# Attention sums one step behind the scores, two activation places, half-step waits, on one Trainium2 core

## The chip, the core and the metric

The kernel runs on one core of a Trainium2 chip. Its engines run side by side and meet at semaphores: TensorE (PE) multiplies matrices into PSUM, ScalarE (ACT) computes activations, VectorE (DVE) does element-wise work and reductions, GpSimd (POOL) does small work and issues some DMAs, and SyncE (SP) issues the others. The metric is the device time of one execution in microseconds (us), and less is better.

## The reference, cut to what matters

One sequence of 2048 rows of 128 features passes an attention layer and a feed-forward layer, each with a residual sum and a layer norm.

```python
x_proj = silu(x @ W1 + b1); u, v, q, k = split(x_proj, 4)      # 16 heads of 8
scores = einsum('bqhd,bkhd->bhqk', qh, kh)
attn = silu(scores) / S                                        # no softmax: S = 2048
av = einsum('bhqk,bkhd->bqhd', attn, vh)
y = layernorm(av * u, gamma, beta) @ W2 + b2                   # x = layernorm(x + y)
h = silu(fp4_linear(x, w_gate)) * fp4_linear(x, w_up)          # 352 features
x = layernorm(x + fp4_linear(h, w_down))                       # fp4: blocks of 16, quantised
```

So 16 x 2048 x 2048 scores have to pass through a SiLU, which only ACT computes, and every one of them is then multiplied with V.

## The kernel before

**Steps.** The queries are cut into ten chunks (`WIDTHS`): six of 256 columns, then four of 128. A step is one block of 128 keys against 1024 columns of scores for each of two halves: for a wide chunk that is two of the four head groups `m`, for a narrow chunk all four. There are 256 steps (`STEPS`), numbered from 0; steps 0 to 191 are wide and 192 to 255 narrow. A wide chunk has 32 steps, a narrow one 16 (`BEGIN` holds their first steps).

**A step on each engine.** PE computes the scores of the step in two half steps (`scores`), each 128x1024 values into a pair of PSUM banks. There are three pairs (`SB`), so half step n waits until ACT has finished half step n-3. ACT turns each pair by one ACTIVATE (line 656) into a place of the tile `attn`, which has `RING` = 3 places of one whole step. PE then multiplies `attn` with a padded V (`times_v`) and adds into one accumulator bank per chunk (`AV`). A step's sum (its "sums" below) is 16 recorded matmuls in a wide chunk and 32 in a narrow one.

**Order on PE.** It is written out (lines 562 to 569): the scores of step `at`, the sums of step `at - LAG` with `LAG` = 2, then at most one job. `times_v` waits once, for both activations of its step (line 464), which two steps behind have long been done.

**Jobs.** The projections of later K, Q, V and u columns and the transposes of the weights are put at fixed steps (`PREP_AT`). Behind the attention of a chunk the other layers of its 128-row tiles are six jobs per tile: `y`, `xqT`, `gate`, `up`, `hqT`, `down` (`TILE_AT`, `EVEN`, `ODD`). Between them DVE normalises and quantises, POOL computes the square root, and ACT runs one SiLU per tile. In a wide chunk tile jobs `down` of an even tile and `y` of an odd one stand one step after the other, as do `hqT` and `down` of an odd tile. The four narrow chunks hold the jobs of tiles 10 to 14, at bases that contain `LAG`. The last tile is computed after the last sums, in the tail, where PE multiplies zeros between its pieces (`keep_warm`). Jobs use the accumulator bank that is not in use (`spare_bank`, which also contains `LAG`), and the sums of a chunk's first step wait for the last job in their bank (`wait_spare`).

Of the kernel before, what the change touches and what calls it, by code (L numbers as in the profile page):

```python
# [12 lines left out]
P = 128  # L13
# [26 lines left out]
def build(nc, x, W1, b1, W2, b2, gamma, beta, w_gate, w_up, w_down, out):  # L40
# [8 lines left out]
    M = 4  # L49
    FEAT = 3  # L50
    PARTS = 5
    TERMS = len(Q_TERMS)
    RING = 3
    SB = 3
    LAG = 2
    WARM_UP = 6
    KEEP_WARM = {"y": 5, "xqT": 27, "gate": 2, "hqT": 22, "down": 2}
    FT = [(0, P), (P, P), (2 * P, FF - 2 * P)]
# [8 lines left out]
    Q0 = [sum(WIDTHS[:c]) for c in range(len(WIDTHS))]  # L67
# [5 lines left out]
    def ms(c, g):  # L73

        per = CH // WIDTHS[c]
        return M_ORDER[g * per:(g + 1) * per]

    AV = [6 + c % 2 for c in range(len(WIDTHS))]

    def spare_bank(at):  # L80

        return 13 - AV[STEPS[at - LAG][0]] if at >= LAG else 7


    PREP_AT = {1: ("v", 1), 3: ("k", 1280), 6: ("v", 2), 8: ("k", 1792), 10: ("v", 3), 12: ("u", 0),
               14: ("q", 256), 16: ("u", 1), 18: ("q", 512), 20: ("u", 2), 22: ("q", 1024), 24: ("u", 3),
               26: ("q", 1536), 28: ("w2", 0), 30: ("gate", 0), 32: ("up", 0), 33: ("down", 0)}

    TAIL = KT - 1
    WIDE, DENSE = KT - 6, KT - 2  # L90
# [3 lines left out]
    for t in range(WIDE, DENSE):  # L94
        TILE_AT[t] = (BEGIN[WIDE // 2 + 1] + LAG + 12 * (t - WIDE),
                      {"y": 0, "xqT": 4, "gate": 5, "up": 7, "hqT": 10, "down": 11})
    TILE_AT[DENSE] = (BEGIN[-2] + LAG, {"y": 0, "xqT": 4, "gate": 6, "up": 8, "hqT": 12, "down": 13})
    JOB_AT = {at: (kind, i, None) for at, (kind, i) in PREP_AT.items()}
# [17 lines left out]
    with ExitStack() as ctx:  # L116
        def sb(name, shape, dt=F32):
            return ctx.enter_context(nc.sbuf_tensor(name, shape, dt))

        def sem(name):  # L120
            return ctx.enter_context(nc.semaphore(name))
# [43 lines left out]
        k_stack = sb("k_stack", [P, SLOTS, S], BF16)  # L165
        q_stack = sb("q_stack", [P, SLOTS, S], BF16)
        attn = sb("attn", [P, RING, 2, 2, CH])
        zu = sb("zu", [P, CH])
# [31 lines left out]
        scores_ready, attn_ready = sem("scores_ready"), sem("attn_ready")  # L200
# [168 lines left out]
        def _(pe):  # L369
            def mm(to, lhsT, rhs, start=True, stop=True):  # L370
                return pe.matmul(to, lhsT, rhs, start=start, stop=stop, skip_group_check=True)  # L371
# [63 lines left out]
            def wait_stacked(c, g, i):  # L435

                if c == g == 0 and ("k", i * P) in unit_no:
                    wait_stack(pe, unit_no[("k", i * P)])
                if g == i == 0 and ("q", Q0[c]) in unit_no:
                    wait_stack(pe, unit_no[("q", Q0[c])])  # L440

            def scores(at):
                c, g, i = STEPS[at]
                w = WIDTHS[c]
                wait_stacked(c, g, i)
                for a in range(2):
                    n = 2 * at + a
                    bank = 2 * (n % SB)
                    if n >= SB:
                        pe.wait_ge(attn_ready, n - SB + 1)  # L450
                    else:
                        pe.wait_ge(head_act, max(head_last[bank], head_last[bank + 1]) + 1)
                    for k, m in enumerate(ms(c, g)):
                        for half in range(2):
                            rows = slice(64 * half, 64 * half + 64)
                            last = mm(ps[:, bank + half, k * w:(k + 1) * w],
                                      k_stack[rows, M * a + m, i * P:(i + 1) * P],
                                      q_stack[rows, M * a + m, Q0[c]:Q0[c] + w])
                    last.then_inc(scores_ready, 1)

            def times_v(at):
                c, g, i = STEPS[at]
                w = WIDTHS[c]
                pe.wait_ge(attn_ready, 2 * (at + 1))
                if c == g == 0 and i % TPC == 0:
                    pe.wait_ge(v_padded, i // TPC + 1)
                if g == i == 0:
                    wait_spare(AV[c], at + LAG)
                for k, m in enumerate(ms(c, g)):
                    for a in range(2):  # L470
                        for half in range(2):
                            cols = slice(32 * (2 * half + a), 32 * (2 * half + a) + 32)
                            last = mm(ps[cols, AV[c], 0:w], v_pad[:, i, m, cols],
                                      attn[:, at % RING, a, half, k * w:(k + 1) * w],
                                      start=(m == M_ORDER[0] and i == 0), stop=(m == M_ORDER[-1] and i == KT - 1))
                last.then_inc(av_done, 1)
# [8 lines left out]
            def wait_spare(bank, at):  # L485

                ks = [k for k, (a, b) in enumerate(zip(sorted(JOB_AT), JOB_BANK)) if b == bank and a < at]
                if ks:
                    wait_job(ks[-1])
                else:  # L490
                    pe.wait_ge(head_act, head_last[bank] + 1)

            def job(at):
# [5 lines left out]
                else:  # L499
                    pe.wait_ge(head_act, head_last[bank] + 1)  # L500
                if at >= BEGIN[1] + LAG:

                    pe.wait_ge(av_taken, STEPS[at - LAG][0])
                if tile is not None:
# [57 lines left out]
            for at in range(len(STEPS)):  # L562
                scores(at)
                if at >= LAG:
                    times_v(at - LAG)
                if at in JOB_AT:
                    job(at)
            for at in range(len(STEPS) - LAG, len(STEPS)):
                times_v(at)
# [29 lines left out]
        def _(act):  # L599
            def silu(to, frm, **kw):  # L600
                return act.activation(to, frm, ACT.Silu, **kw)  # L601
# [47 lines left out]
            for at in range(len(STEPS)):  # L649
                for a in range(2):  # L650
                    n = 2 * at + a
                    act.wait_ge(scores_ready, n + 1)
                    if a == 0 and at >= RING:
                        act.wait_ge(av_done, at - RING + 1)
                    b = 2 * (n % SB)
                    silu(attn[:, at % RING, a, :, :], ps[:, b:b + 2, :]).then_inc(attn_ready, 1)
                    if a == 0 and at - 1 in JOB_AT:
# [16 lines left out]
        def _(dve):  # L674
# [78 lines left out]
            def take_av(c):  # L753
# [3 lines left out]
                for tile in range(TAIL):  # L757
                    if chunk_of(tile) == c - 1:
                        dve.wait_ge(job_made, job_no[("y", 0, tile)] + 1)
                dve.scalar_tensor_tensor(out=zu[:, 0:w], in0=ps[:, AV[c], 0:w], scalar=1.0 / S,  # L760
                                         in1=uT[:, Q0[c]:Q0[c] + w], op0=ALU.mult, op1=ALU.mult).then_inc(av_taken, 1)
# [198 lines left out]
```

## Time and profile before

| | |
|---|---|
| median of 3 runs | 524.06 us (523.19 to 524.69) |
| the profiled execution | 523.96 us |
| its span (first to last instruction) | 522.2 us |
| busy: ACT | 490.9 us, 94% |
| busy: PE | 502.7 us, 96% |
| busy: weight loads (PEld) | 265.5 us, 51% |
| busy: DVE | 212.3 us, 41% |
| busy: POOL | 56.6 us, 11% |
| granted PE clock, mean | 0.996 |

The span leaves 1.8 us of the execution outside. Busy time on PE is modelled at the end of each matmul, so starts of instructions are the safer numbers there. A timeline view merges a run of equal instructions into one row and gives the idle time before it in brackets. Its ACT rows contain activations that overlap at their edges. Of the page's chain of waits, ACT has 50% and PE 32%, and its issue share is 13%.

### The profile page before, as it was taken

Reading aid. Unit: us, or ns where it says so; the run is one execution under the profiler, and the core shown is the slowest. Engines: PE = TensorE matmul, PEld = TensorE weight load, DVE = VectorE, ACT = ScalarE, POOL = GpSimd, SP = SyncE. Lnnn points to the kernel's source line nnn. Section 1 sums busy time; section 2 is a strip of 40 time slices with the busy share of each in tenths; the row PEclk is TensorE's granted clock in tenths of the full one; section 3 lists DMA queues with packets and bytes.
Section 4 is the critical chain, followed back from the end, with each engine's and each line's share of the span. In section 5 each row is a group of like instructions: output and inputs, shape, how many; then the busy total and the mean of one; then the engine's idle time right before and its main releaser. Section 6 shows DMA issues by size and latency. Waiting matters only on the chain.

```text
span 522.2 us, 20050 instructions
## 1 busy us (share of the span) xinstructions
PE 502.7 (96%) x9054; PEld 265.5 (51%) x9056; DVE 212.3 (41%) x624; ACT 490.9 (94%) x557; POOL 56.6 (11%) x148
## 2 busy tenths in 40 slices
PE   8899999999999999999999999999999999999996
PEld 5454334444444434444443444444477777777753
DVE  5447742332433432243433432243434354544344
ACT  5899999999999999999999999999999999999920
POOL 7700001010010101001010100001010110101010
PEclk9899999999999999999999999999999999999999
DMA  7831450000000000000000000000000000000000
GB/s 186 203 94 48 107 141 4 1 8 3 6 3 1 8 2 8 3 1 8 2 8 1 8 1 8 3 3 8 1 9 4 9 9 5 9 3 9 4 8 6
DMA packets 15155, 12.38 MB, mean 24 GB/s; under 512 B 1783, under 2 KB 14718, under 8 KB 15070
## 3 DMA queue, kind: packets, MB, share of 16 engines
q1 hardware_dynamic: 14088, 9.44, 6.9%
q0 software_dynamic: 688, 1.40, 1.1%
q8 instruction: 71, 1.16, 0.9%
q10 hardware_dynamic: 294, 0.26, 0.2%
q14 instruction: 14, 0.11, 0.1%
HBM read 1.92 MB, written 1.05 MB: 6 GB/s over the span
## 4 chain that ended last, share of the span: by engine, by line
ACT 50%; PE 32%; issue 13%; DVE 2%; POOL 1%; DMA 1%; POOLq 0%; DVEq 0%; ACTq 0%
ACT attn L601 50%; PE ps L371 30%; PE ps L385 2%; DMA q_stack<-parts 1%; POOL rstd_b L359 1%; PE ps L414 0%; DVE stats_b L764 0%; ACT feat L601 0%; POOL ve_b L358 0%; DVE mv_b L766 0%; ACT v_sb L601 0%; DVE x_b L769 0%; DVE x1p_b L774 0%; DVE xn_b L742 0%; DVE xn_b L743 0%
## 5 line engine op out<-in xcount | busy, mean ns | idle before, releaser
L601 ACT ACTIVATE attn<-ps 128x1024 f32<-128x1024 f32 x512 | 478.8, 1191 | 3.4 <-PE ps L371 3.1
L371 PE MATMUL ps<-attn,v_pad 128*32 128x256 f32 (+1 forms) x5120 | 274.5, 341 | 0.4 <-ACT attn L601 0.3
L371 PE MATMUL ps<-q_stack,k_stack 64*128 64x256 bf16 (+1 forms) x2560 | 174.1, 251 | 10.9 <-ACT attn L601 1.4
L371 PEld LDWEIGHTS ps<-attn,v_pad 128*32 128x32 f32 x5120 | 132.4, 109 | 80.4 <-issue 38.9
L371 PEld LDWEIGHTS ps<-q_stack,k_stack 64*128 64x128 bf16 x2560 | 78.5, 94 | 135.1 <-ACT attn L601 90.6
L358 POOL TENSOR_TENSOR ve_a<-mv_a,eps_col 128x1 f32<-128x1 f32 x24 | 4.6, 191 | 264.2 <-DVE mv_a L766 264.2
L814 DVE TENSOR_TENSOR gate_a<-gate_a,ps 128x352 f32<-128x352 f32 x8 | 4.2, 522 | 55.4 <-PE ps L371 55.4
L358 POOL TENSOR_TENSOR ve_b<-mv_b,eps_col 128x1 f32<-128x1 f32 x24 | 4.6, 192 | 175.6 <-DVE mv_b L766 175.6
L814 DVE TENSOR_TENSOR gate_b<-gate_b,ps 128x352 f32<-128x352 f32 x7 | 3.7, 522 | 47.0 <-PE ps L371 47.0
L371 PE MATMUL ps<-zeros 128*128 128x512 bf16 (+1 forms) x63 | 16.1, 403 | 1.3 <-DVE zeros L835 1.2
L701 DVE CAST parts<-feat 128x512 bf16<-128x512 f32 (+1 forms) x10 | 3.7, 373 | 26.8 <-ACT feat L601 26.8
L359 POOL TENSOR_TENSOR rstd_a<-ve_a,minus_half 128x1 f32<-128x1 f32 x24 | 13.2, 552 | 1.9
L359 POOL TENSOR_TENSOR rstd_b<-ve_b,minus_half 128x1 f32<-128x1 f32 x24 | 13.2, 551 | 1.9
L371 PE MATMUL ps<-wgate_t,xqT 128*32 128x352 f32 (+1 forms) x122 | 12.5, 460 | 0.2 <-ACT xqT L662 0.2
L371 PE MATMUL ps<-wup_t,xqT 128*32 128x352 f32 (+1 forms) x122 | 12.4, 459 | 0.0
L769 DVE TENSOR_SCALAR x_a<-x1p_a,mv_a,rstd_a 128x128 f32<-128x128 f32 x16 | 5.5, 347 | 15.0 <-POOL rstd_a L359 15.0
L769 DVE TENSOR_SCALAR x_b<-x1p_b,mv_b,rstd_b 128x128 f32<-128x128 f32 x16 | 5.5, 346 | 15.0 <-POOL rstd_b L359 15.0
L822 DVE COPY hqT_a<-ps 128x256 f32<-128x256 f32 x8 | 3.4, 425 | 19.2 <-PE ps L385 19.2
L828 DVE TENSOR_TENSOR x1p_a<-ps,x_a 128x128 f32<-128x128 f32 x8 | 2.3, 292 | 21.2 <-PE ps L371 21.2
L371 PEld LDWEIGHTS ps<-zeros 128*128 128x128 bf16 x65 | 6.4, 102 | 8.7 <-issue 1.7
L764 DVE BATCH_NORM_STATS2 stats_a<-ps 128x6 f32<-128x128 f32 x8 | 2.4, 298 | 19.1 <-PE ps L371 19.1
L601 ACT ACTIVATE feat<-ps,b_col 128x512 f32<-128x512 f32 (+1 forms) x10 | 7.5, 746 | 2.5 <-PE ps L371 2.5
(152 smaller groups left out, 346.9 us busy)
## 6 DMA issues: line engine op xcount, KB each, us to landing
q_stack<-parts SPq DMA_DIRECT2D x18, 128.0 KB, 2.4
k_stack<-parts SPq DMA_DIRECT2D x15, 128.0 KB, 3.5
x_sb<-in_L_attn_x SPq DMA_DIRECT2D x3, 256.0 KB, 4.6
k_stack<-zeros SPq DMA_DIRECT2D x6, 128.0 KB, 4.8
q_stack<-zeros SPq DMA_DIRECT2D x6, 128.0 KB, 2.9
k_stack<-parts SPq DMA_DIRECT2D x9, 64.0 KB, 2.1
q_stack<-parts SPq DMA_DIRECT2D x9, 64.0 KB, 2.9
out<-x_a SPq DMA_DIRECT2D x8, 64.0 KB, 1.6
```

Source lines behind the costliest of these rows:

```text
L358: link(pool.tensor_tensor(r.ve[:, :], r.mv[:, which, 1:2], eps_col[:, :], ALU.add))
L359: pool.tensor_tensor(r.rstd[:, which:which + 1], r.ve[:, :], minus_half[:, :], ALU.pow).then_inc(rstd_ready, 1)
L371: return pe.matmul(to, lhsT, rhs, start=start, stop=stop, skip_group_check=True)
L385: return pe.transpose(ps[0:m, bank, a:a + n], src[:, 0:m], ident[0:n, 0:n])
L601: return act.activation(to, frm, ACT.Silu, **kw)
L701: dve.tensor_copy(p[:, 0, :], f).then_inc(split_done, 1)
L764: dve.bn_stats(r.stats[:, :], src)
L769: return dve.tensor_scalar(to, src, r.mv[:, which, 0:1], r.rstd[:, which:which + 1], ALU.subtract, ALU.mult)
L814: dve.tensor_tensor(r.gate[:, :], r.gate[:, :], ps[:, bank, 0:FF], ALU.mult).then_inc(job_by_vec, 1)
L822: dve.tensor_copy(r.hqT[:, 0:2, :].rearrange("p t n -> p (t n)"), ps[:, bank, 0:2 * P])
L828: dve.tensor_tensor(r.x1p[:, :], ps[:, bank, 0:D], r.x1[:, :], ALU.add).then_inc(job_by_vec, 1)
```

## The change

`LAG` goes from 2 to 1 and `RING` from 3 to 2. The new function `group` lets a half step hold half of the `m` with both halves `b` of the stacks, where before it held all `m` with one. With that a half step of `attn` feeds a complete half of the step's sums, and `times_v` waits for each half of the activations by itself. Three weight transposes now stand at steps 30, 31 and 32 in place of 30, 32 and 33. Through `LAG` the jobs of tiles 10 to 14 stand one step earlier, and the bank of a job is chosen for the step before it.

```diff
-    RING = 3
+    RING = 2
     SB = 3
-    LAG = 2
+    LAG = 1
...
+    def group(c, g, a):
+
+        some = ms(c, g)
+        return [(m, b) for m in some[a * len(some) // 2:(a + 1) * len(some) // 2] for b in range(2)]
+
...
-               26: ("q", 1536), 28: ("w2", 0), 30: ("gate", 0), 32: ("up", 0), 33: ("down", 0)}
+               26: ("q", 1536), 28: ("w2", 0), 30: ("gate", 0), 31: ("up", 0), 32: ("down", 0)}
...
-                    for k, m in enumerate(ms(c, g)):
+                    for k, (m, b) in enumerate(group(c, g, a)):
                         for half in range(2):
                             rows = slice(64 * half, 64 * half + 64)
                             last = mm(ps[:, bank + half, k * w:(k + 1) * w],
-                                      k_stack[rows, M * a + m, i * P:(i + 1) * P],
-                                      q_stack[rows, M * a + m, Q0[c]:Q0[c] + w])
+                                      k_stack[rows, M * b + m, i * P:(i + 1) * P],
+                                      q_stack[rows, M * b + m, Q0[c]:Q0[c] + w])
...
-                pe.wait_ge(attn_ready, 2 * (at + 1))
...
-                for k, m in enumerate(ms(c, g)):
-                    for a in range(2):
+                for a in range(2):
+                    pe.wait_ge(attn_ready, 2 * at + a + 1)
+                    for k, (m, b) in enumerate(group(c, g, a)):
                         for half in range(2):
-                            cols = slice(32 * (2 * half + a), 32 * (2 * half + a) + 32)
+                            cols = slice(32 * (2 * half + b), 32 * (2 * half + b) + 32)
```

The order of instructions on PE shows it in three places. In these rows `q_stack,k_stack` are scores, `attn,v_pad` are sums, and `attn_ready` is ACT's count of finished half steps. The first place is step 1 and the start of step 2, before; `w1_sb,xT` and `b1v_parts,ones_bf16` are the projection of V for keys 512 to 1023:

```order
29 L371 MATMUL ps<-q_stack,k_stack 128x256 [waits attn_ready]
30 L371 MATMUL ps<-q_stack,k_stack 128x256 x3
31 L371 MATMUL ps<-w1_sb,xT 32x128 [waits head_act]
32 L371 MATMUL ps<-w1_sb,xT 32x128 x15
33 L371 MATMUL ps<-b1v_parts,ones_bf16 32x512 x4
34 L371 MATMUL ps<-q_stack,k_stack 128x256 [waits attn_ready,stacked_by_pool2,stacked2]
```

The same place on PE in the changed kernel:

```order
30 L376 MATMUL ps<-q_stack,k_stack 128x256 x3
31 L376 MATMUL ps<-attn,v_pad 32x256 [waits attn_ready,head_act,v_padded]
32 L376 MATMUL ps<-attn,v_pad 32x256 x3
33 L376 MATMUL ps<-attn,v_pad 32x256 [waits attn_ready]
34 L376 MATMUL ps<-attn,v_pad 32x256 x3
35 L376 MATMUL ps<-w1_sb,xT 32x128 [waits head_act]
36 L376 MATMUL ps<-w1_sb,xT 32x128 x15
37 L376 MATMUL ps<-b1v_parts,ones_bf16 32x512 x4
38 L376 MATMUL ps<-q_stack,k_stack 128x256 [waits attn_ready,stacked_by_pool2,stacked2]
```

The sums of step 0 now stand ahead of that projection and of the scores of step 2. The second place is PE at the end of the program before, from the job `down` of tile 14 to the zeros that open the tail:

```order
1805 L371 MATMUL ps<-wdown_t,hqT_a 32x128 [waits av_taken,job_by_vec]
1806 L371 MATMUL ps<-wdown_t,hqT_a 32x128 x11
1807 L371 MATMUL ps<-attn,v_pad 32x128 [waits attn_ready]
1808 L371 MATMUL ps<-attn,v_pad 32x128 x15
1809 L371 MATMUL ps<-attn,v_pad 32x128 [waits attn_ready]
1810 L371 MATMUL ps<-attn,v_pad 32x128 x15
1811 L371 MATMUL ps<-zeros 128x512 x5
```

And in the changed kernel:

```order
2310 L376 MATMUL ps<-wdown_t,hqT_a 32x128 x11
2311 L376 MATMUL ps<-q_stack,k_stack 128x128 [waits attn_ready]
2312 L376 MATMUL ps<-q_stack,k_stack 128x128 x7
2313 L376 MATMUL ps<-q_stack,k_stack 128x128 [waits attn_ready]
2314 L376 MATMUL ps<-q_stack,k_stack 128x128 x7
2315 L376 MATMUL ps<-attn,v_pad 32x128 [waits attn_ready]
2316 L376 MATMUL ps<-attn,v_pad 32x128 x7
2317 L376 MATMUL ps<-attn,v_pad 32x128 [waits attn_ready]
2318 L376 MATMUL ps<-attn,v_pad 32x128 x7
2319 L376 MATMUL ps<-attn,v_pad 32x128 [waits attn_ready]
2320 L376 MATMUL ps<-attn,v_pad 32x128 x7
2321 L376 MATMUL ps<-attn,v_pad 32x128 [waits attn_ready]
```

The last scores now stand behind that `down`, and each of the last two sums is split in two, each half with its own wait. The third place is PE at steps 31 and 32 of the changed kernel, where the transposes of two weights follow the sums directly (`wup_n` and `wdown_n` are the weights):

```order
309 L376 MATMUL ps<-attn,v_pad 32x256 [waits attn_ready]
310 L376 MATMUL ps<-attn,v_pad 32x256 x3
311 L390 MATMUL ps<-ident,wup_n 128x128 [waits wq_ready,job_by_vec]
312 L390 MATMUL ps<-ident,wup_n 128x128
313 L390 MATMUL ps<-ident,wup_n 128x96
314 L376 MATMUL ps<-q_stack,k_stack 128x256 [waits attn_ready,stacked6]
315 L376 MATMUL ps<-q_stack,k_stack 128x256 x3
```

Before, a step without a job stood between the transposes of `wgate_n` and of `wup_n`.

## Rows read from the trace of the kernel before

**Rows 1.** The page, its costliest group: busy us, mean ns, idle us before, releaser

```profile
L601 ACT ACTIVATE attn<-ps 128x1024 f32<-128x1024 f32 x512 | 478.8, 1191 | 3.4 <-PE ps L371 3.1
```

**Rows 2.** Timeline, PE and its weight loads, a wide stretch: start, length, instructions

```profile
208.74 0.83 PE L371 MATMUL ps<-attn,v_pad 128*32 128x256 f32 x12
...
209.50 0.11 PEld L371 LDWEIGHTS ps<-q_stack,k_stack 64*128 64x128 bf16 x4 [0.41 <-ACT attn L601]
210.00 0.11 PEld L371 LDWEIGHTS ps<-q_stack,k_stack 64*128 64x128 bf16 x4 [0.39 <-ACT attn L601]
210.33 0.59 PEld L371 LDWEIGHTS ps<-attn,v_pad 128*32 128x32 f32 x16 [0.21 <-issue]
211.33 0.11 PEld L371 LDWEIGHTS ps<-q_stack,k_stack 64*128 64x128 bf16 x4 [0.41 <-ACT attn L601]
```

**Rows 3.** Timeline, all engines, the first scores and their activations

```profile
14.10 0.83 PE L371 MATMUL ps<-q_stack,k_stack 64*128 64x256 bf16 x12 [1.33 <-DMA q_stack<-parts]
14.53 3.77 ACT L601 ACTIVATE attn<-ps 128x1024 f32<-128x1024 f32 x4 [1.03 <-PE ps L371]
...
15.61 0.48 PE L371 MATMUL ps<-q_stack,k_stack 64*128 64x256 bf16 x4 [0.68 <-ACT attn L601]
```

**Rows 4.** Timeline, PE, score blocks around two bursts of a wide chunk

```profile
107.57 0.90 PE L371 MATMUL ps<-q_stack,k_stack 64*128 64x256 bf16 x8
...
115.71 0.61 PE L371 MATMUL ps<-q_stack,k_stack 64*128 64x256 bf16 x8
...
135.43 0.90 PE L371 MATMUL ps<-q_stack,k_stack 64*128 64x256 bf16 x8
...
139.94 0.61 PE L371 MATMUL ps<-q_stack,k_stack 64*128 64x256 bf16 x8
```

**Rows 5.** Timeline, PE, score blocks around bursts of the narrow chunks

```profile
399.06 0.89 PE L371 MATMUL ps<-q_stack,k_stack 64*128 64x128 bf16 x16
...
405.59 0.62 PE L371 MATMUL ps<-q_stack,k_stack 64*128 64x128 bf16 x16
...
433.01 0.89 PE L371 MATMUL ps<-q_stack,k_stack 64*128 64x128 bf16 x16
...
437.48 0.62 PE L371 MATMUL ps<-q_stack,k_stack 64*128 64x128 bf16 x16
...
474.14 0.43 PE L371 MATMUL ps<-ident,zu 128*32 128x128 f32 x8 [0.98 <-DVE zu L760]
```

**Rows 6.** Timeline, PE, wide chunk: the first weight transpose and the scores around it

```profile
76.05 0.90 PE L371 MATMUL ps<-q_stack,k_stack 64*128 64x256 bf16 x8
...
78.33 0.61 PE L371 MATMUL ps<-q_stack,k_stack 64*128 64x256 bf16 x8
```

**Rows 7.** Timeline, all engines, steps 0 to 2

```profile
16.02 1.93 PE L371 MATMUL ps<-w_sb,xT 128*32 128x128 f32 x32
...
18.31 1.03 PE L371 MATMUL ps<-q_stack,k_stack 64*128 64x256 bf16 x8
18.96 1.02 ACT L601 ACTIVATE attn<-ps 128x1024 f32<-128x1024 f32 x1 [0.66 <-PE ps L371]
```

**Rows 8.** Busy time by stretch: bounds, length, then PE, PEld, DVE, ACT, POOL, granted clock, DMA share, GB/s

```profile
16.00:17.00 1.00, 1.00 (x22) 0.92 (x24) 0.75 (x1) 1.00 (x2) 1.00 (x3) 0.50 1.04 267
19.00:20.00 1.00, 1.00 (x20) 0.42 (x16) 0.00 (x0) 1.00 (x2) 1.00 (x2) 0.90 1.25 249
```

**Rows 9.** Timeline, PE, steps 6 and 7: the projection of V for keys 1024 on

```profile
27.81 1.06 PE L371 MATMUL ps<-w_sb,xT 128*32 128x128 f32 x32
...
29.02 0.61 PE L371 MATMUL ps<-q_stack,k_stack 64*128 64x256 bf16 x8
29.56 1.07 PE L371 MATMUL ps<-attn,v_pad 128*32 128x256 f32 x16
```

**Rows 10.** Timeline, ACT and PE, the last activations and sums

```profile
494.50 4.94 ACT L601 ACTIVATE attn<-ps 128x1024 f32<-128x1024 f32 x5
...
500.93 1.03 PE L371 MATMUL ps<-zeros 128*128 128x512 bf16 x4 [0.16 <-issue]
```

## The prediction

> **What bounds the kernel now.** I read four views: the page's groups, the timeline of one undisturbed wide stretch, the timeline around each place where ACT stands, and the two ends. The group of the score activations tells the most: 478.8 us busy, with only 3.4 us idle ahead of all 512 of them [rows 1]. A score activation costs half of the period of the undisturbed steps, (211.33 - 209.50) / 2 = 0.917 us [rows 2]. So ACT is the bound, and each us for which it stands is lost for good; PE, which shows a busy share of 96% on the page, matters only when its scores come too late.
>
> How late may they come? In the undisturbed stretch the first score pair starts at 209.50, the second at 210.00 after a wait for ACT, the sums at 210.33, and the next scores at 211.33 [rows 2]. A waiting pair starts 0.05 us after the activation that frees it: 14.53 + 1.02 = 15.55, against 15.61 [rows 3]. The activation that freed the second pair thus ended at 209.95, and the one before it at 209.03; the first pair starts 0.47 us after that end. A pair that ACT waits for is in use 0.43 us after its start, and its activation ends 1.02 us later [rows 3]. To keep ACT running, the pair's activation has to end three periods after the one that freed it, at 211.78, so the pair could start as late as 211.78 - 1.45 = 210.33. **PE has 0.83 us of room** at the first pair of an undisturbed step. It gives up part of it with each job and wins back, per step, 1.83 less its own work: the scores of a step without a wait take 29.56 - 29.02 = 0.54 [rows 9], the sums 211.33 - 210.33 = 1.00, which leaves 0.29 us.
>
> The two bursts of a wide pair of tiles show how near the edge that is. From 107.57 to 115.71 are four steps and 8.14 us, 0.80 more than 4 x 1.834; from 135.43 to 139.94 are two steps, 0.84 more than 3.67 [rows 4]. The first leaves 0.03 of room, the second overruns it by about 0.015. In the narrow chunks 399.06 to 405.59 are three steps and 1.03 too long, so ACT stands for 0.2; 433.01 to 437.48 are two steps and 0.80 too long [rows 5].
>
> **The change part by part.**
>
> *The late half of the sums.* The same matmuls run, in the same shapes and number, so PE's work per step stays 1.54 us. What moves is when it may run. The sums' second half now waits for the activation that also frees the next first pair. It starts 0.05 after that end, and the scores only after it. Of a sum of 1.00 us the last three of four rounds take 209.50 - 208.74 = 0.76 [rows 2], so one round is 0.24 or a little less and the last two take 0.54. The first pair then starts 0.05 + 0.54 = 0.59 us after the freeing end in place of 0.47. I take a shift of 0.13 us; the room shrinks from 0.83 to 0.70. The price is paid once in each burst that begins from an undisturbed step, and only as far as the burst's delay exceeds the rest: delay + 0.13 - 0.83. Bounds: 0 if the second half starts at once, beside the drain of the first; 0.24 if the restart costs a round more. In steps without a job this costs nothing, since 0.13 of PE's 0.29 idle us simply move.
>
> - Wide, `down` then `y`: 0.80 + 0.13 - 0.83 = 0.10, in five chunks (those of tiles 0 to 9): 0.5.
> - Wide, `hqT` then `down`: overrun already, so the whole 0.13, five times: 0.65.
> - Narrow, `down` then `y`: ACT stands already, 0.13 each at tiles 10/11, 11/12, 12/13 and 13/14: 0.5. At the last of these PE waits another 0.98 us for VectorE's `zu` [rows 5], behind that engine's work on `down`; both move along with PE, so that wait stays.
> - Narrow, `xqT` then `gate`, tiles 11 to 13, by tile 12's 0.80: 0.11 each, 0.3.
>
> *The job table.* One transpose delays the scores by 78.33 - 76.05 - 1.83 = 0.45 [rows 6]. Three in a row delay by 3 x 0.45 - 2 x 0.29 = 0.77. The sums of step 32 then wait for the copy of the third, as they do now, some 0.35 net of what is won back: up to 0.84. Cost 0.84 + 0.13 - 0.83 = 0.15; with the steps 30, 32 and 33 it was nothing.
>
> *The last `down`.* It now stands ahead of the last scores. With `hqT` before it this is the burst of 0.8 to 0.9 again: 0.87 + 0.13 - 0.83 = 0.17.
>
> *The start.* Here ACT has already stood 0.66 us for the third step's scores, which wait behind the projection of V [rows 7]. The changed order puts the sums of step 0 ahead of it. They can start where the projection starts now, at 16.02. What they cost depends on the clock. From 16 us on PE runs at a granted 0.50, 1.2 GHz, after it had stood 1.33 us for a DMA and 0.68 us for ACT [rows 3, 8]; 19 to 20 us shows 0.90, so it returns to 2.4 GHz near 19.2. The same projection takes 18.31 - 16.02 = 2.29 us there and 1.21 us at full clock [rows 7, 9]. Sums at half clock are then 1.9 us, by the same ratio, to about 18.0. The projection gets 1.2 us of its 2.29 before 19.2, the rest takes 0.6: scores at 19.8. ACT follows 0.43 later at full clock, and its activation ends at 21.27 in place of 18.96 + 1.02 = 19.98: **+1.29**. The bounds are -0.3 (full clock throughout: 16.0 + 1.0 + 1.2 = 18.2, and a shorter lead), and about +3 (half clock through the next steps too).
>
> The next bursts have no room either. The later end of the first activations makes the second half of the sums of step 2 wait, ahead of the projection of K: about 0.17. The projection of V at step 6 stands ACT already and adds 0.13. That at step 10 adds 0.04.
>
> The Trainium skill (TensorE: Matmul & The Clock Gate, section on what you observe) says that the point at which the clock changes moves from run to run. By it the start would cost between nothing and 1.3 us, run by run; no row here shows a second run's clock. The sum is made without it.
>
> *The end.* ACT ends at 494.50 + 4.94 = 499.44, and the zeros that follow the last sums start at 500.93 [rows 10]: both last sums stand there, the first of them held up by `down`. In the changed order only the second half of one is left: 499.44 + 0.05 + 0.55 = 500.04, **-0.89**. The five zeros and `zu` then set the tail as now.
>
> *Ring of two places.* ACT's first activation of a step waits for the sums two steps back. PE has issued these ahead of the very scores that it needs, so this wait never ends last: nothing.
>
> **Sum.** 0.5 + 0.65 + 0.5 + 0.3 + 0.15 + 0.17 = 2.3 for the bursts, 1.29 + 0.34 = 1.6 for the start, -0.9 for the end: +3.0 to +3.1. On the profiled execution of 523.96 us, 0.1 below the median, that gives 527.1.
>
> **Rivals.**
>
> *A, the start alone.* The second half's wait costs no room, because PE's spare 0.29 us takes it up before each burst. For it: nothing in the undisturbed steps gets longer. Against it: the overruns of rows 4 and 5 start from undisturbed steps and are counted from the first pair. Then 1.3 - 0.9 + 0.3 = +0.7: 524.7, no change to be told.
>
> *B, not slower by the clock.* The stretch at half clock disappears or shrinks. The sums of step 0 cost 1.0, the projection gets 1.1 cheaper, and the start term is -0.3; it decides if PE's clock is at 2.4 GHz from 16.1 us on. With all burst terms: 3.1 - 1.6 = +1.5, 525.5, just within what can be told. Against it: everything up to 16 us is unchanged, the 1.33 us idle too.
>
> *C, dearer restarts.* The half that waits pays a round more, a shift of 0.24. About 18 bursts then pay 0.11 more, +2.0: 529.1. It would also follow from the clock staying low longer at the start (+1.7 at most). Against it: the second score pair, which restarts after a wait, takes 210.33 - 210.00 = 0.33 [rows 2], close to the 0.27 that is half of a block without one.
>
> **How the numbers follow.** Forecast 0.66, A 0.10, B 0.08, C 0.13, and 0.03 for something faster that I don't see. A change of 0.3%, 1.6 us, is about what a measurement of this kernel can tell. Slower takes the forecast, C, and a little of B: 0.83. Same takes A and most of B: 0.14. Faster: 0.03. The range runs from 525.4 (B) to 528.8 (short of C): it leaves out A and most of C.
>
> **What would show it.** ACT's first long idle should be near 1.9 us with the sums of step 0 ahead of it in place of 0.66. ACT's idle before score activations should grow from 3.4 to about 7.3 us. In undisturbed wide steps PE should show two waits per step, at the second scores pair and inside the sums, the first scores 0.6 us after the end that frees them, with the period still 1.83. After the wide bursts rows of ACT should break where they now run through. The zeros of the tail should start 0.6 us after ACT's last end. The forecast is wrong if the shift is near 0, if the start costs under 0.5 us, or if ACT breaks in steps without a job.

## The result, and the profile after

| | before | changed |
|---|---|---|
| median | 524.05 us (4 runs, 523.19 to 524.69) | 529.53 us (4 runs, 528.84 to 529.56) |
| ratio to before | | 1.0098, 95% interval 1.0079 to 1.0117 |
| profiled execution, span | 522.2 us | 527.7 us |

The changed kernel is slower by 5.5 us. The forecast was slower by 3.1 us, 527.1 us in a range of 525.4 to 528.8: the right side, but too small. The score activations on the page of the changed kernel, which answer to [rows 1] (busy us, mean ns, then idle before them and its releasers; the lines below line 74 have moved down by five):

```profile
L606 ACT ACTIVATE attn<-ps 128x1024 f32<-128x1024 f32 x512 | 477.1, 1104 | 7.0 <-PE ps L376 5.1
```

The idle ahead of ACT's 512 activations doubles, from 3.4 to 7.0 us. In the chain of waits on the page PE has 82% in place of 32%. That share is a rough sign only: e4 below, with the changed kernel's time and nearly its idle, has 51% there.

Undisturbed wide steps answer to [rows 2]; this is the timeline of the weight loads of the changed kernel, with the start and the idle time before each row:

```profile
94.73 0.11 PEld L376 LDWEIGHTS ps<-q_stack,k_stack 64*128 64x128 bf16 x4 [0.41 <-issue]
95.07 0.11 PEld L376 LDWEIGHTS ps<-q_stack,k_stack 64*128 64x128 bf16 x4 [0.23 <-ACT attn L606]
95.40 0.16 PEld L376 LDWEIGHTS ps<-attn,v_pad 128*32 128x32 f32 x8 [0.21 <-issue]
95.99 0.16 PEld L376 LDWEIGHTS ps<-attn,v_pad 128*32 128x32 f32 x8 [0.44 <-ACT attn L606]
96.56 0.11 PEld L376 LDWEIGHTS ps<-q_stack,k_stack 64*128 64x128 bf16 x4 [0.41 <-issue]
```

The step still lasts 96.56 - 94.73 = 1.83 us. The second half of the sums waits at 95.99, 0.05 after the activation that frees it, and the next scores start at 96.56. That is 0.62 us behind the end of that activation, where it was 0.47: a shift of 0.15 to 0.16, with 0.13 forecast. The half costs 0.57, not 0.54.

The start of the changed kernel, PE and ACT in two pieces of the timeline, answers to [rows 7]:

```profile
16.22 1.94 PE L376 MATMUL ps<-attn,v_pad 128*32 128x256 f32 x16 [0.22 <-POOL v_pad L338]
17.93 1.84 PE L376 MATMUL ps<-w_sb,xT 128*32 128x128 f32 x32
19.59 0.39 PE L376 MATMUL ps<-b1v_parts,ones_bf 96*32 96x512 bf16 x4
19.92 0.61 PE L376 MATMUL ps<-q_stack,k_stack 64*128 64x256 bf16 x8
```

```profile
20.35 1.02 ACT L606 ACTIVATE attn<-ps 128x1024 f32<-128x1024 f32 x1 [2.05 <-PE ps L376]
```

The sums of step 0 and the projection stand ahead of the scores of step 2, as forecast: scores at 19.92 (19.8 forecast), ACT idle 2.05 us (about 1.9 forecast). The sums start 0.2 later than forecast, behind a wait for the padded V that the forecast left out, and are then shorter (1.71 us to the projection, 1.9 forecast). PE's clock was again low there, from stretches of the trace that answer to [rows 8] (the granted clock is the third number from the end):

```profile
16.00:17.00 1.00, 0.78 (x8) 0.40 (x12) 0.62 (x2) 1.00 (x2) 1.00 (x3) 0.56 1.08 268
19.00:20.00 1.00, 1.00 (x24) 0.65 (x16) 0.00 (x0) 0.00 (x0) 1.00 (x3) 0.73 0.97 236
```

**Where the 5.5 us are.** From the ends of the 512 score activations in both traces one gets, for each, the time over the 0.917 us of an undisturbed one (and over ACT's own jobs). This is the time for which ACT stands, and "stands" below means this sum. It is up to 0.1 us more at each place than the idle of the timeline, because an activation that has waited takes 1.02 us to its end, and one in a stream 0.917. Summed by place, in us:

| place | before | changed | more | forecast |
|---|---|---|---|---|
| step 2 | 0.77 | 2.16 | 1.39 | 1.29 |
| steps 4 and 7 | 0.26 | 0.61 | 0.35 | 0.30 |
| step 11 | 0 | 0.42 | 0.42 | 0.04 |
| steps 13 to 29, eight places | 0 | 1.48 | 1.48 | 0 |
| steps 32 and 33 | 0 | 0.23 | 0.23 | 0.15 |
| wide, `down` then `y`, five | 0 | 0.67 | 0.67 | 0.5 |
| wide, `hqT` then `down`, five | 0.08 | 0.89 | 0.81 | 0.65 |
| narrow chunks to step 242 | 2.31 | 2.97 | 0.66 | 0.8 |
| step 255, the last `down` | 0 | 0.21 | 0.21 | 0.17 |
| after ACT's last score activation | 22.70 | 22.06 | -0.64 | -0.89 |
| sum | | | 5.6 | 3.0 |

Two rows hold nearly three quarters of the miss of 2.6: step 11, and the eight places from 13 to 29. All the others are off by 0.25 or less, but the row of the narrow chunks hides two errors that nearly cancel. Behind `down` and `y` it has 0.68 more in place of 0.5, and behind `xqT` and `gate` nothing in place of 0.3.

**What happens at these places.** The timeline of PE in the changed kernel, around the projection of step 22 (`xT,w_qk`):

```profile
63.11 0.64 PE L376 MATMUL ps<-attn,v_pad 128*32 128x256 f32 x8
64.02 0.64 PE L376 MATMUL ps<-attn,v_pad 128*32 128x256 f32 x8 [0.28 <-ACT attn L606]
64.48 1.04 PE L376 MATMUL ps<-xT,w_qk 128*32 128x512 f32 x8
65.45 0.61 PE L376 MATMUL ps<-q_stack,k_stack 64*128 64x256 bf16 x8
```

and of ACT in the same kernel:

```profile
62.38 0.68 ACT L606 ACTIVATE uT<-ps,b_col 128x512 f32<-128x512 f32 x1
62.95 3.96 ACT L606 ACTIVATE attn<-ps 128x1024 f32<-128x1024 f32 x4
66.81 0.68 ACT L606 ACTIVATE feat<-ps,b_col 128x512 f32<-128x512 f32 x1
```

ACT's own job, the SiLU of the last projection (`uT`), stands between the two activations of the step. So the second activation ends 0.57 us later than in an undisturbed step, at 63.97, and the second half of the sums waits for it. Behind that half PE has the next projection (0.86 us), and only then the scores. They start 0.05 + 0.57 + 0.86 = 1.48 us behind the end that freed them. ACT needs them by 1.30 (three periods less the 1.45 us of lead), so it should stand for 0.18; the ends of its activations give 0.19. From the end of `uT` (62.38 + 0.68) to that of `feat` (66.81 + 0.68), two steps and one such job, it is 4.43 us.

Before, the same stretch, PE's piece of the timeline and then ACT's:

```profile
59.92 1.07 PE L371 MATMUL ps<-attn,v_pad 128*32 128x256 f32 x16
60.81 1.04 PE L371 MATMUL ps<-xT,w_qk 128*32 128x512 f32 x8
61.79 0.61 PE L371 MATMUL ps<-q_stack,k_stack 64*128 64x256 bf16 x8
```

```profile
59.08 1.04 ACT L601 ACTIVATE uT<-ps,b_col 128x512 f32<-128x512 f32 x1
59.65 4.13 ACT L601 ACTIVATE attn<-ps 128x1024 f32<-128x1024 f32 x4
63.27 1.09 ACT L601 ACTIVATE feat<-ps,b_col 128x512 f32<-128x512 f32 x1
```

The sums two steps back waited for nothing, so PE spent the time of ACT's job on the projection. From the end of `uT` (59.08 + 1.04) to that of `feat` (63.27 + 1.09) it was 4.24 us, 0.19 less. (Ends are compared here, since ACT's rows overlap at their starts by amounts that differ.)

### The profile page after: what moved, and what is told of

It reads as the page before. It is cut to its first block, busy times and chain, and to the rows that moved or that the text cites. A ratio compares the mean times of both kernels' runs of the same rounds, so it can differ in the third digit from the quotient of the medians.

```text
span 527.7 us, 20051 instructions
## 1 busy us (share of the span) xinstructions
PE 512.5 (97%) x9054; PEld 257.1 (49%) x9056; DVE 211.9 (40%) x624; ACT 493.4 (93%) x557; POOL 56.6 (11%) x148
## 3 DMA queue, kind: packets, MB, share of 16 engines
HBM read 1.92 MB, written 1.05 MB: 6 GB/s over the span
## 4 chain that ended last, share of the span: by engine, by line
PE 82%; ACT 11%; issue 3%; POOL 2%; DVE 2%; POOLq 0%; ACTq 0%; DVEq 0%
PE ps L376 80%; ACT attn L606 10%; PE ps L390 2%; POOL k_stack L246 1%; POOL v_pad L338 0%; ACT feat L606 0%; POOL rstd_b L364 0%; POOL q_stack L246 0%; ACT gate_a L606 0%; DVE stats_b L769 0%; ACT gate_b L606 0%; ACT uT L606 0%; ACT v_sb L606 0%; POOL ve_b L363 0%; DVE mv_b L771 0%
## 5 line engine op out<-in xcount | busy, mean ns | idle before, releaser
L376 PE MATMUL ps<-attn,v_pad 128*32 128x256 f32 (+1 forms) x5120 | 295.0, 344 | 5.8 <-ACT attn L606 3.7
L376 PEld LDWEIGHTS ps<-attn,v_pad 128*32 128x32 f32 x5120 | 119.4, 109 | 118.9 <-ACT attn L606 62.6
L376 PE MATMUL ps<-q_stack,k_stack 64*128 64x256 bf16 (+1 forms) x2560 | 164.5, 250 | 1.9 <-DMA q_stack<-parts 1.2
L376 PEld LDWEIGHTS ps<-q_stack,k_stack 64*128 64x128 bf16 x2560 | 82.7, 94 | 112.0 <-ACT attn L606 62.7
L376 PE MATMUL ps<-xT,w_qk 128*32 128x512 f32 (+3 forms) x56 | 9.6, 538 | 0.0
```

## The experiments

Each kernel is compared with runs of the kernel before on the same chip, made beside it; a ratio is that of the medians, with its 95% interval. There is one trace of each kernel. Start terms are read with care, because the first 20 us differ between traces even where PE's program is the same (last section).

**e1, ACT's job behind both activations.** The changed kernel with

```diff
-                    if a == 0 and at - 1 in JOB_AT:
+                    if at - 1 in JOB_AT and a == (1 if JOB_AT[at - 1][2] is None else 0):
```

> The changed kernel, but ACT's SiLU of a projection (k, q, v, u) runs after the second score activation of its step in place of after the first. Theory, coupling with ACT's jobs: from step 4 to 29 ACT stands because the second half of the sums waits for an activation that ACT's own job of 0.36 to 0.57 us has delayed, and PE's next projection is queued behind that half. With the job behind both activations the idle of step 4 (0.19 us), of steps 13 to 29 (eight places, 1.48 us) and most of that of step 11 (0.42 to about 0.06) go: 2.0 us, from 529.5 to 527.5. Rival, dearer restarts: the waiting half costs more after a wait wherever it stands, so the idle stays: 529.5. The first idle of 2.2 us and step 7 (0.42) stay under both.

Measured: 527.62 us (5 runs), ratio 1.0063 (1.0047 to 1.0078), 1.9 us less than the changed kernel. Its slowest run is below the fastest of the changed kernel. ACT no longer stands at steps 4, 13 to 29 and 32. At step 11 it stands for 0.07, at step 7 still for 0.42, at step 33 for 0.13. Its ACT, by the timeline:

```profile
60.98 0.93 ACT L606 ACTIVATE uT<-ps,b_col 128x512 f32<-128x512 f32 x1
61.55 4.02 ACT L606 ACTIVATE attn<-ps 128x1024 f32<-128x1024 f32 x4
65.21 0.93 ACT L606 ACTIVATE feat<-ps,b_col 128x512 f32<-128x512 f32 x1
```

The two steps take 4.23 us from end to end (60.98 + 0.93 to 65.21 + 0.93), against 4.43. No work was taken out and PE's program is the changed one. The restart of the waiting half is untouched, so dearer restarts are not the cause of these 2 us.

**e2, the projections ahead of the sums.** The changed kernel with, in PE's loop,

```diff
                 scores(at)
+                ahead = at in JOB_AT and JOB_AT[at][2] is None
+                if ahead:
+                    job(at)
                 if at >= LAG:
                     times_v(at - LAG)
-                if at in JOB_AT:
+                if at in JOB_AT and not ahead:
                     job(at)
```

> The changed kernel, but the jobs of the preparation (projections and weight transposes) stand ahead of the sums of their step on PE, behind the scores. Theory, coupling: the same idle goes by the other way, since no projection is queued behind the waiting half: steps 4, 11, 13 to 29 and 32, 33 lose about 0.19 + 0.36 + 1.48 + 0.23, step 7 some 0.16: 2.4 us, to 527.1. The first idle stays at 2.2 us, because sums of step 0 and projection both still stand ahead of the scores of step 2. Rival, dearer restarts: nothing of it changes but the order of equal work, 529.5. Rival, clock: if PE's lower clock at 16 to 19 us were behind the excess, 529.5 as well.

Measured: 527.33 us (6 runs), ratio 1.0060 (1.0044 to 1.0076) and its slowest run too is below the fastest of the changed kernel. In its trace ACT does not stand at step 4 and from 11 to 33, and at step 7 for 0.27, the 0.26 of before. At step 2 it stands for 1.88 us. The same loss goes by the other end of the coupling: ACT's order is the changed one here, PE's is not.

**e3, two steps behind until step 38.**

```diff
-    RING = 2
+    RING = 3
...
-                if at >= LAG:
-                    times_v(at - LAG)
+                if 2 <= at <= 38:
+                    times_v(at - 2)
+                if at >= 38:
+                    times_v(at - 1)
```

> The changed kernel, but with three activation places and the sums two steps behind until step 38, where two steps' sums run, and one step behind from there. Theory: all that the change costs in the start and the preparation goes, 1.39 + 0.19 + 0.16 + 0.42 + 1.48 + 0.23 = 3.9 us, and the catching up at step 38 makes ACT stand for about 0.2: 525.8. Wide and narrow bursts and the tail stay as in the changed kernel. Rival, that the cost is spread over all 256 steps: it would give back 38/256 of 5.5 us, 0.8 us, and 528.7.

Measured: 526.4 us (7 runs, 524.79 to 527.96), ratio 1.0043 (1.0027 to 1.0059): 3.1 us less than the changed kernel in place of 3.7. The trace has of steps 3 to 33 only the 0.26 of step 7, and 0.04 at step 39. By place 3.8 us should be gone (1.4 at the start, 2.4 behind it), 0.7 more than by the medians. The spread of this kernel's runs can hold that, but it was not separated. A cost spread evenly over the steps (528.7) is excluded; 38 of 256 steps hold more than half of it.

**e4, three places.** The changed kernel with `RING = 3`, nothing else.

> The changed kernel with three activation places in place of two and nothing else. Theory: ACT's wait for the sums two steps back never ends last, since PE issues them ahead of the scores that ACT waits for anyway: 529.5, no change. Rival, places: if ACT or PE is held by the missing place anywhere, this gives time back, and ACT's idle before its score activations falls below the 7.0 us of the changed kernel.

Measured: 529.22 us, ratio 1.0097 (1.0081 to 1.0113). From step 4 on ACT stands as in the changed kernel, at every place within 0.03 us. The missing place costs nothing there. (At step 2 it stands for 1.06 us in place of 2.16, with another clock, see the last section.)

**e5, one wait for the whole sum.**

```diff
-                for a in range(2):
-                    pe.wait_ge(attn_ready, 2 * at + a + 1)
+                pe.wait_ge(attn_ready, 2 * (at + 1))
+                for a in range(2):
```

> The changed kernel, but the sums wait for both activations of their step before the first matmul, still one step behind. Theory, room: the first scores of an undisturbed step then start about 1.08 us after the activation that frees them in place of 0.62, which leaves 0.2 us of room in place of 0.67. Nearly every job (0.22 to 1.09 us long) then makes ACT stand: about 3.3 us per pair of tiles in the wide chunks in place of 0.3, and more in the preparation and the narrow chunks, in all some 20 to 30 us, 545 to 560. Undisturbed steps keep a period of 1.83 us. Rival, the cost follows the late work itself: 0.46 us more in each of 256 steps, 118 us.

Measured: 555.88 us, ratio 1.0613 (1.0585 to 1.0640). This is the hardest test of the reckoning by room, since nearly every job now overruns. The trace shows PE's weight loads in undisturbed steps:

```profile
101.00 0.33 PEld L376 LDWEIGHTS ps<-q_stack,k_stack 64*128 64x128 bf16 x8 [0.41 <-ACT attn L606]
101.84 0.59 PEld L376 LDWEIGHTS ps<-attn,v_pad 128*32 128x32 f32 x16 [0.50 <-ACT attn L606]
102.84 0.33 PEld L376 LDWEIGHTS ps<-q_stack,k_stack 64*128 64x128 bf16 x8 [0.41 <-ACT attn L606]
```

The step keeps its 1.84 us. The first scores start 1.05 us behind the end that frees them (102.84 against 101.84 - 0.05), which leaves 0.25 us of room; the expectation had 0.2. In the wide chunks ACT stands for 0.36 us at each `gate` and each `up`, 0.20 at each even `y` and 0.24 at each `hqT`, but not at `xqT`. That is 14.6 us for steps 34 to 191, where 3.3 x 5 = 16.5 was expected. So the split waits, taken alone, are worth 26 us one step behind.

**e6, the halves two steps behind.** The changed kernel with `LAG = 2`, `RING = 3` and the job table of before; left of the change are `group` and the two waits.

> The kernel before with the new grouping and the two half-step waits, but two steps behind and three places (and the weight transposes where they were). Theory: the halves never wait two steps behind, so regrouping and splitting cost nothing: 524.0 as before. Rival, regrouping: the new order of the stationary matrices, or a second wait per step, costs PE time: scores and sums of a step take more than 1.54 us together, and the time lies over 524.5.

Measured: 524.11 us (12 runs), ratio 1.0002 (0.9990 to 1.0015). Regrouping and the second wait cost nothing that can be measured, and with e4 the ring is out as well. The loss is left to the sums one step behind, together with the job table at steps 32 and 33 (0.23 us). No run has the one step behind with the old table, so these two are not separated.

**e7, the sums of step 0 behind the scores of step 2.** The changed kernel with `RING = 3` and

```diff
-                if at >= LAG:
+                if at == 2:
+                    times_v(0)
+                if at >= 2:
                     times_v(at - LAG)
```

> The changed kernel, but the sums of step 0 run behind the scores of step 2 (three places), all later ones as in the changed kernel. Theory: ACT's first idle falls from 2.2 (1.1 with a full clock) to the 0.7 or less of the kernel before, and step 3 has to take the sums of two steps and stands for about 0.4: 528.5, with the start's own spread of about 1 us between runs. Rival: if the first idle came from the wait for padded V or for the clock alone, it stays over 1 us.

Measured: 528.74 us (4 runs), ratio 1.0095 (1.0068 to 1.0123). In its trace ACT does not stand at step 2 and stands for 0.43 at step 4. Its PE had full clock there, though, where the changed order stands for only 0.42 at step 2 (e1's trace). At full clock the traces thus show that the sums of step 0 ahead of the scores make ACT stand. The size of 1.39 us at half clock is not tested: the two medians lie 0.8 apart with overlapping ranges (527.95 to 531.19, and 528.84 to 529.56).

**e8, one step behind in the last chunk alone.** The kernel of e6 with

```diff
+            CLOSE = BEGIN[-2] + LAG
...
-                if at >= LAG:
+                if LAG <= at <= CLOSE:
                     times_v(at - LAG)
+                if at >= CLOSE:
+                    times_v(at - 1)
...
-            for at in range(len(STEPS) - LAG, len(STEPS)):
-                times_v(at)
+            times_v(len(STEPS) - 1)
```

> The kernel before (two steps behind, three places) with the halves, but one step behind from step 242 on, in the last chunk alone; the extra sums of step 241 stand there ahead of the job y of tile 14, in the 0.98 us for which PE waits for VectorE. Theory: catching up is free there, the last sums end about 0.6 us earlier, and VectorE's work on tile 14 then sets the tail: 0.3 to 0.5 us less than before, 523.6. Rival: the late half costs as much in the last chunk as the tail gives back: 524.0. Rival, no cover: the sums of step 241 push y and the next scores later: 524.5 to 525.

Measured: 523.85 us (11 runs), ratio 0.9993 (0.9980 to 1.0006): not told from before. In the trace catching up is free (ACT stands for 1.38 at step 243, as before), and what follows ACT's last score activation takes 22.45 us, where the three traces with two steps behind at the end (before, e6, e9) have 22.69 to 22.70. The gain of the tail is small, and only the trace shows it. PE waits 0.32 us for VectorE's `zu` there.

**e9, the accumulator first.** Not part of the change: it goes for the largest idle behind the start, which both kernels share. The kernel before with

```diff
-                if at - LAG in BEGIN:
-                    take_av(BEGIN.index(at - LAG) - 1)
+                if at - LAG + 1 in BEGIN:
+                    take_av(BEGIN.index(at - LAG + 1) - 1)
```

> The kernel before, but VectorE takes the finished accumulator of a chunk (zu) one step earlier in its program: at the end of the chunk before tile 14 it stands ahead of the work behind down of tile 13, not behind it. Not part of the change; it goes for the longest single idle of ACT behind the start that both kernels share, 1.39 us at step 243, while PE waits 0.98 us for zu. Theory: the job y of tile 14 then waits for nothing, that idle shrinks to the 0.17 us of the other such places: 1.2 us less than before, 522.8. Rival: VectorE's work on down comes later and holds the accumulator bank that y needs, and the idle stays: 524.0.

Measured: **522.58 us** (12 runs), ratio 0.9978 (0.9962 to 0.9995), against 523.83 us of before beside it. The place that answers to the last of [rows 5], PE in its timeline:

```profile
471.21 1.08 PE L371 MATMUL ps<-attn,v_pad 128*32 128x128 f32 x32
472.09 0.42 PE L371 MATMUL ps<-ident,zu 128*32 128x128 f32 x8
472.31 0.42 PE L371 MATMUL ps<-w_centred,zu 128*32 128x128 f32 x8
472.66 0.62 PE L371 MATMUL ps<-q_stack,k_stack 64*128 64x128 bf16 x16
```

The job `y` follows the sums with no wait for `zu`, and ACT stands for 0.19 at step 243 in place of 1.39. This is the only version whose interval lies below the kernel before, by 0.2%, and it owes nothing to the change.

## Why the prediction was right and wrong

**The bound** was right: ACT. The time for which it stands in the two traces, with the tail, sums to the difference of the spans within 0.1 us.

**The step that failed** is "I take a shift of 0.13 us ... The price is paid once in each burst that begins from an undisturbed step". It was worked out where the two activations of a step follow each other directly, and then used for every burst. In the preparation ACT has a job between them, so that the second half of the sums waits 0.57 us longer, and PE's own next job is queued behind that half. I read room from rows of steps without ACT's jobs, and gave steps 13 to 29 no term, step 11 one of 0.04. Measured there are 1.9 us in place of 0.04. e1 takes them away by ACT's order (all but 0.07), e2 by PE's. The prediction had the same coupling once, for the projection of K at step 3 (0.17, measured 0.19), but put it down to the late start alone.

**The size of the shift** was 0.16, not 0.13: the last two rounds of the sums and the change to the scores take 0.57. Over ten wide bursts this is 0.3 us, the rest of their miss.

**The narrow chunks** were near by luck, 0.66 in place of 0.8. At the four `down` and `y` ACT stands for 0.15, 0.15, 0.24 and 0.14 more, in place of 0.13 each. At `xqT` and `gate` the 0.11 each did not come. The 0.80 of tile 12 contained a wait for VectorE: before, the transposes start at 434.97, 0.15 behind the end of VectorE's last work on `xn_a`. In the changed kernel that wait takes up the shift, and the two steps are 0.63 too long (436.96 to 441.26), which still fits the room.

**The start** was right in its mechanism and near in size for the profiled run: 1.39 against 1.29. That two traces with the stretch at half clock were compared is luck, for with PE's same order ACT stands for 0.42 (e1), 1.06 (e4) or 2.16 us at this place. e1's 0.42 less the 0.77 of before is -0.35, close to the bound of -0.3 for full clock. As rival B said, the stretch at half clock can be absent. But the traces with the order of before and full clock, e6 and e9, stand for 0 and 0.16 there, so at equal clock the change costs time at the start all the same. No trace of the kernel before itself has full clock there.

**The end** gave back 0.64, not 0.89. The last half of the sums to the first of the zeros is 505.72 to 506.53, 0.81 us, not 0.55: the 0.43 us from the start of the last round to that of the first matmul on zeros belongs to it, and the 0.55 had no room for that. The timeline of PE in the changed kernel:

```profile
505.72 0.64 PE L376 MATMUL ps<-attn,v_pad 128*32 128x128 f32 x16 [0.27 <-ACT attn L606]
506.30 0.76 PEld L376 LDWEIGHTS ps<-zeros 128*128 128x128 bf16 x5 [0.20 <-issue]
506.53 1.03 PE L376 MATMUL ps<-zeros 128*128 128x512 bf16 x4 [0.16 <-issue]
```

**The ring, the job table and the last `down`** were right: nothing (e4), 0.23 against 0.15, and 0.21 against 0.17.

**A sign that misled.** The prediction asked for an idle of about 7.3 us before the score activations, and 7.0 came, while the time was 2.4 us off. The 7.3 was reckoned as standing time. The page's idle leaves out up to 0.1 us at each place and counts the idle before the very first activation (1.03 us before, 0.89 after). By the ends, ACT stands for 3.4 us before and 9.6 after.

**The rivals.** A (no cost by the shift) is excluded by the ten wide bursts. C named a time of 529.1, close to the measured one, for a reason that is wrong: restarts cost 0.03 more, not a round. The measured time lies above the predicted range, because the range held only sizes of the terms that were named, and nothing for a place where the one shift would not apply.

## What to carry to other kernels

- A wait that is moved nearer to its producer should be reckoned at each kind of step, not in the undisturbed one alone: what else does the producer run just before the awaited instruction, and what does the waiting engine have queued behind it? Here the two were each hidden alone (e1, e2) and cost 0.12 to 0.42 us together.
- For an engine with spare time, the number to know is the room at the point where the bound engine needs it (0.83 us of a step of 1.83), and the bursts of work that come near it. In the changed kernel, with 0.16 us less room and the coupling above, ACT stands at 34 places in place of 11. With about 0.6 less nearly each job makes it stand (e5).
- Where sums must follow closely, let the work that waits for nothing go ahead of the half that waits (e2).

## What the runs showed of the hardware

PE's clock in the first 20 us differs between executions of equal code. The changed kernel and e1 have the same program on PE. In e1's trace the clock between 16 and 20 us is granted in full, and ACT idles 0.32 us for the scores of step 2. In that of the changed kernel the granted clock is 0.57 over these 4 us (0.50, which is 1.2 GHz, from 17 to 19), and the idle is 2.05 us. This stretch of e1:

```profile
16.00:20.00 4.00, 3.40 (x72) 1.95 (x76) 2.66 (x3) 3.68 (x5) 4.00 (x8) 1.00 1.13 232
```

What PE did before does not tell the two apart. These are the first scores, with the idle before them, of e1 and then of the changed kernel:

```profile
15.09 0.83 PE L376 MATMUL ps<-q_stack,k_stack 64*128 64x256 bf16 x12 [1.38 <-DMA q_stack<-parts]
14.10 0.83 PE L376 MATMUL ps<-q_stack,k_stack 64*128 64x256 bf16 x12 [1.18 <-DMA q_stack<-parts]
```

Both then idle 0.68 us more for ACT. The one with the longer idle kept its clock. So the prediction's argument against rival B, that everything up to 16 us is unchanged, does not hold.

e4, with PE's same order, had 0.95 us of idle and a granted clock of 0.72 in these 4 us. The Trainium skill (TensorE: Matmul & The Clock Gate, section on what you observe) says that the point of the change varies from run to run, by half a microsecond either way. These traces agree that it varies, and show more: in e1 the stretch at half clock is absent altogether, which goes with 1.7 us less idle of ACT. In e8, whose start has the order of before, it is longer: the granted clock is 0.50 from 16 to 20 us and 0.68 from 20 to 24, and ACT stands for 1.9 us at steps 2 to 4, where the kernel before stands for 0.77.

The end of the first score activation also moves, from 15.2 us (e3) to 16.6 us (e2). The two together may be why the runs of one kernel spread over 0.7 to 3.3 us here; that is not shown, since each kernel has one trace. From step 8 on, places of equal order repeat within 0.03 us between traces. So a difference of 1 us is seen better in the standing of ACT by place than in a median of five runs.
